# Gated slot attention block on one core: a second home for the high and low halves of two head weights, made one and two slots before the change of head

## What is computed

```
q = silu(causal_conv4(h @ Wq));  k, v, w likewise            # 16 heads of 128
g = log_sigmoid(h @ Wf1 @ Wf2);  beta = sigmoid(h @ Wb);  w = l2norm(w)
scan over the 512 tokens, per head:
    Sk = Sk * exp(g) + k (beta w)^T ;  Sv = Sv * exp(g) + (beta w) v^T
    o  = softmax(q Sk / sqrt(128)) Sv
o = rms_norm(o) * norm_w * sigmoid(h @ Wg1 @ Wg2 + bg2)
x = layernorm(x + o @ Wo);  x = layernorm(x + ffn(x))
```

## Time and profile before

| what | value |
|---|---|
| median of three executions | 2012.46 us |
| the profiled execution, device time | 2009.03 us |
| its span in the profile | 2007.3 us |
| PE busy | 1927.6 us, 96% |
| PE weight loads | 1627.1 us, 81% |
| DVE busy | 1775.8 us, 88% |
| ACT busy | 1396.5 us, 70% |
| POOL busy | 1334.0 us, 66% |
| chain that ended last, by engine | PE 82%, POOL 8%, DVE 5%, issue 3%, ACT 1%, DMA 1% |
| granted TensorE clock, mean | 0.984 of full speed |

### The profile page before, as it was taken

One profiled execution on the slowest core, in us unless ns is written; L12 is line 12 of the kernel. 1 busy time (PEld: TensorE's weight loads), 2 busy tenths in 40 slices (PEclk: granted clock), 3 DMA queues, 4 the chain that ended last, 5 costly groups with the idle time before them and its releaser, 6 DMA issues.

```text
span 2007.3 us, 41500 instructions
## 1 busy us (share of the span) xinstructions
PE 1927.6 (96%) x12192; PEld 1627.1 (81%) x12192; DVE 1775.8 (88%) x4096; ACT 1396.5 (70%) x3986; POOL 1334.0 (66%) x2289
## 2 busy tenths in 40 slices
PE   7899999999999999999999999999999999999697
PEld 5688888888888888888888888888888888887586
DVE  5599999999999999999999999999999999998487
ACT  4477777777777777777777777777777777776442
POOL 5367676767677676777677776777676766766343
PEclk8899999999999999999999999999999999999798
DMA  3011110111111111111111111111110111102300
GB/s 78 1 55 26 25 35 14 36 24 33 26 24 26 26 34 23 27 24 32 26 27 23 27 34 24 26 24 33 26 34 15 29 32 23 22 15 51 63 11 32
DMA packets 53645, 58.51 MB, mean 29 GB/s; under 512 B 14896, under 2 KB 44720, under 8 KB 53424
## 3 DMA queue, kind: packets, MB, share of 16 engines
q0 software_dynamic: 9216, 33.56, 11.4%
q1 hardware_dynamic: 44208, 22.29, 4.0%
HBM read 20.19 MB, written 37.75 MB: 29 GB/s over the span
## 4 chain that ended last, share of the span: by engine, by line
PE 82%; POOL 8%; DVE 5%; issue 3%; ACT 1%; DMA 1%; POOLq 0%; DVEq 0%; ACTq 0%
PE proj_ps L718 15%; PE mix_ps L802 11%; PE V_ps L773 10%; PE work_ps L927 8%; PE work_ps L933 7%; PE tr_ps L742 6%; PE V_ps L751 5%; PE work_ps L1569 5%; PE proj_ps L397 4%; PE work_ps L822 3%; PE mix_ps L809 2%; POOL w_lo L370 2%; PE tr_ps L782 2%; PE work_ps L824 2%; POOL qk L618 1%
## 5 line engine op out<-in xcount | busy, mean ns | idle before, releaser
L587 DVE SCALAR_TENSOR_TENSOR conv<-proj_ps,coefs,conv 128x511 f32<-128x511 f32 (+2 forms) x768 | 561.9, 732 | 9.5 <-ACT conv L347 2.6
L298 POOL TENSOR_TENSOR W<-W,tot 128x256 f32<-128x256 f32 x384 | 256.0, 667 | 244.0 <-PE mix_ps L802 243.9
L1053 POOL TENSOR_TENSOR A_lev<-A,masks 128x256 f32<-128x256 f32 x448 | 319.5, 718 | 0.1
L802 PE MATMUL mix_ps<-W,U 128*128 128x128 f32 x1792 | 295.3, 287 | 13.7 <-POOL W L298 8.2
L802 PEld LDWEIGHTS mix_ps<-W,U 128*128 128x128 f32 x1792 | 256.5, 192 | 40.2 <-issue 24.5
L773 PE MATMUL V_ps<-A_lev,UT 128*128 128x128 f32 x1792 | 285.9, 282 | 1.6 <-DVE V_ps L683 1.6
L711 DVE COPY_PREDICATED A<-masks,mix_ps 128x256 f32<-128x256 uint32 x448 | 268.7, 600 | 12.3 <-PE mix_ps L802 12.2
L580 DVE TENSOR_TENSOR wT<-wT,tot 128x128 f32<-128x128 f32 x768 | 233.3, 344 | 40.3 <-DVE U L563 1.8
L773 PEld LDWEIGHTS V_ps<-A_lev,UT 128*128 128x128 f32 x1792 | 237.4, 192 | 23.4 <-DVE V_ps L683 23.2
L356 ACT ACTIVATE th<-conv 128x512 f32<-128x512 f32 x256 | 162.3, 634 | 104.2 <-DVE conv L587 103.0
L718 PE MATMUL proj_ps<-hT_hi,w_hi 128*128 128x512 f32 x512 | 222.9, 435 | 4.5 <-DVE conv L587 2.7
(11 more groups left out here) (200 smaller groups left out, 4774.0 us busy)
## 6 DMA issues: line engine op xcount, KB each, us to landing
head_sum<-y_sb POOLq DMA_DIRECT2D x64, 512.0 KB, 6.5
w_raw<-in_L_attn_Ww SPq DMA_DIRECT2D x16, 128.0 KB, 2.2
w_raw<-in_L_attn_Wq SPq DMA_DIRECT2D x16, 128.0 KB, 2.2
w_raw<-in_L_attn_Wk SPq DMA_DIRECT2D x16, 128.0 KB, 2.3
w_raw<-in_L_attn_Wv SPq DMA_DIRECT2D x16, 128.0 KB, 2.2
wo_raw<-in_L_attn_Wo SPq DMA_DIRECT2D x16, 128.0 KB, 2.0
head_sum<-in_L_attn_hidden_states SPq DMA_DIRECT2D x1, 2048.0 KB, 10.3
acc<-head_sum SPq DMA_DIRECT2D x4, 512.0 KB, 3.9
```

The costliest lines, as they stand in the source:

```text
L298: nc.gpsimd.tensor_tensor(w, w, block_tot(u3.par, lev, 0), ALU.mult).then_inc(W_step, 1)
L587: nc.vector.scalar_tensor_tensor(y_, proj_ps[:, CONV_BANK[i], 0:T - back], filt(u, i, KW - 1 - back), y_, ALU.mult, ALU.add).then_inc(conv ...
L802: last = nc.tensor.matmul(mix_ps[:, half, p * P:(p + 1) * P], Ulev(u3, lev)[:, p * P:(p + 1) * P], after_odd(W[:, p * T // 2:(p + 1) * T / ...
L1053: nc.gpsimd.tensor_tensor(dst, diag_after_odd(lev), mask_cols(lev), ALU.mult)\
```

## The change

For odd heads the halves of Ww and Wq (i < 2) live in the first 512 columns of `setup_hi_sb` and `setup_lo_sb`; for even heads in `w_hi` and `w_lo` as before. The two homes alternate, so the halves of the next head can be made while the present head is still in use. Ww's halves are now made in the slot n % 4 = 1, two slots sooner than before, and Wq's in the slot n % 4 = 2, one slot sooner; for head 1 both are made in slot 2, when the first products are done. ACT makes the high half at r = 3 as before, POOL the low half after `fac` as before. The halves of Wf2 and Wk stay where they were, in the slot n % 4 = 3, that of Wv in the slot n % 4 = 0. Two waits guard the buffers: on `proj_ps_ready` for the end of head h-2, and for head 1 on `raw_ps`.

```
+        def half(main, other, h, i):
+
+            if h % 2 and i < 2:
+                return other[:, i * KT * P:(i + 1) * KT * P].rearrange("p (k n) -> p k n", k=KT)
+            return main[:, i]
+
         def high_weights(act, h, i):
 
             act.wait_ge((head_w, head_q, head_k, head_v)[i], 16 * (h + 1))
-            nc.scalar.activation(w_hi[:, i], w_raw[:, i], ACT.Copy).then_inc(high_done, 1)
+            if h and i < 2:
+                wait(act, proj_ps_ready, 5 * B * (h - 1))
+            if h == 1 and i == 0:
+                act.wait_ge(raw_ps, B)
+            nc.scalar.activation(half(w_hi, setup_hi_sb, h, i), w_raw[:, i], ACT.Copy).then_inc(high_done, 1)
 
         def low_weights(pool, h, i):
 
             pool.wait_ge(high_done, 4 * h + i + 1)
-            nc.gpsimd.tensor_tensor(w_lo[:, i], w_raw[:, i], w_hi[:, i].bitcast(F32),
+            nc.gpsimd.tensor_tensor(half(w_lo, setup_lo_sb, h, i), w_raw[:, i], half(w_hi, setup_hi_sb, h, i).bitcast(F32),
                                     ALU.subtract).then_inc(low_done, 1)
+
+        def ahead(s):
+
+            if not s.u1 or s.u1.h + 1 == H:
+                return ()
+            return {1: (0,) if s.u1.h else (), 2: (1,) if s.u1.h else (0, 1)}.get(s.u1.par, ())
...
-            split_product(proj_ps[:, CONV_BANK[i], :], w_hi[:, i], w_lo[:, i],
+            split_product(proj_ps[:, CONV_BANK[i], :], half(w_hi, setup_hi_sb, u.h, i), half(w_lo, setup_lo_sb, u.h, i),
...
+                for i in ahead(s):
+                    low_weights(pool, u1.h + 1, i)
                 if s.next_h:
-                    low_weights(pool, s.next_h, 0)
                     low_f(pool, s.next_h)
-                    low_weights(pool, s.next_h, 1)
                     low_weights(pool, s.next_h, 2)
...
+                    if r == 3:
+                        for i in ahead(s):
+                            high_weights(act, u1.h + 1, i)
                     if s.next_h and r == 3:
                         act.wait_ge(proj_ps_ready, u1.count(5, 3))
                         high_f(act, s.next_h)
-                        high_weights(act, s.next_h, 0)
-                        high_weights(act, s.next_h, 1)
```

## The result

The changed kernel took 2016.39 us (median of 12 executions, 2014.26 to 2018.48), the kernel before 2012.16 us (12 executions on the same chips, 2008.47 to 2014.18). The ratio is 1.0022, with a 95% interval of 1.0013 to 1.0031. The profiled execution took 2014.42 us (span 2012.7), that of the kernel before 2009.03 (span 2007.3).

A forecast was written before the change was run, and what follows sets the result against it. DVE, its scalings and copies held up by POOL, was taken to decide slot length at L751 behind a change of head. Terms of 3.5 + 0.7 = +4.2 us on the median 2012.46 gave 2016.6 us, range 2010.8 to 2019.5.

The forecast's parts named there:

- slot 20: First slot of head 5, 28.33 us before; forecast like other changes of head, with L751 at +0.25 us.
- slot 56: Slot behind a change of head, 28.63 us before; already has such a collision, so L751 was to change by -0.04.
- POOL is free at once, and the wait for qk goes: At a new head, L618 starts 0.17 us into the slot; PE's 15 waits of 0.43 us go.
- The wait is worth only 0.05 us a head: At each change of head, taking away PE's wait for qk alone would win 0.05 us, not 0.34.
- The pair is held up and DVE comes 0.30 us later: New head's start: scaling pair L580 falls behind POOL's q product; taps start at 600.88 instead of 600.58.
- L751 at +0.25 us for 14 heads, 3.5 us: PE's second product into V_ps starts at 605.70 instead of 605.45 in slot 20; +3.5 us for 14 changes of head.
- Slots n % 4 = 3, +0.7 us: `w_lo` at the end of slots n % 4 = 2 makes `largest` about 0.2 us late; 0.05 us for each of 15.
- ACT and SP at nothing: ACT's high halves in slots n % 4 = 1 and 2 are covered, SP's order stays; no cost counted.
- The wait for qk was the bound: Rival: at changes of head L751 goes back to 9.07 us; -5.4 us, 2007.1 us; chance 0.11.
- The pair gets in first: Rival: DVE's first scaling passes before L618, taps start as now; between -0.8 and +0.7 us, 2012.5 us; chance 0.20.
- The halves are not made sooner: Rival: a raw weight or a wait comes late, so POOL waits for ACT; about 2012.5 us; chance 0.02.

The follow-up runs named there:

- Ww only: The changed kernel, but only Ww's halves are made early and Wq's stay in the slot n % 4 = 3: 2010.69 us, ratio 0.9999 to the kernel before.
- the gate products alone: The kernel before, with the gate products of levels 4 and 5 made at i == 4, except in slots n % 4 = 2: 2008.65 us, ratio 0.9985.
- the order alone: The kernel before, with DVE's scaling of level 3 put ahead of `largest` at the change of head: 2018.88 us, ratio 1.0038.
- The first experiment: The changed kernel, with DVE's scaling of level 3 put ahead of `largest` at the change of head: 2005.77 us, ratio 0.9976 to the kernel before.
- three fillers: The changed kernel plus three POOL instructions writing an unread spare tile, at the end of the slot before a new head: 2012.24 us, ratio 1.0003 to the kernel before.
- the two fillers: The changed kernel plus two POOL instructions writing an unread spare tile, in place of the two `w_lo` taken away: 2015.69 us, ratio 1.0027 to the kernel before.

## Why the prediction was right, point by point

**The total.** Forecast 2016.6 us, measured 2016.39 against 2012.16; +4.2 us forecast over the kernel before, +4.2 measured between the medians. That the two agree so closely is in part luck, since the interval of the ratio allows 2.6 to 6.2 us. In the profiled executions the difference is 5.4 us, and the slots, +5.6 together, show what the sum had wrong: slot 20 costs 0.9 us more than I gave it, slot 56 0.2 more, the slots n % 4 = 1 and 2, which I had at nothing, 0.6, and the slots n % 4 = 3 0.3 less. The mechanism is the forecast one: the held pair makes up 3.3 us of it, in the 13 changes of head other than those at slots 20 and 56.

**POOL is free at once, and the wait for qk goes.** Right: L634 at 0.17 us, L943 at 2.62, no wait. **The wait is worth only 0.05 us a head.** Right: 0.04 us in the experiment with Ww only, and 4.79 - 4.73 = 0.06 in the table.

**The pair is held up and DVE comes 0.30 us later.** Right: 1.54 us for a forecast of 1.53; "DVE done" goes from 4.62 to 4.92. What the prediction didn't say is that the kernel before already lost 0.76 us there to the same two instructions; it was contained in the measured start of the taps, so the sum held. Had I listed it, the likely gain of another order would have been plain: the pair only has to be ahead of the q product. The Trainium skill, SBUF — State Buffer, section "SBUF: two separate sides", has whole instructions wait in turn for a pair of ports, and the traces agree: what is held ends about 0.14 us behind the half of the q product that it waited for. With the gate products alone, a half that ends at 712.02 + 0.75 = 712.77 gives 712.91, and the copy ends at 712.04 + 0.87 = 712.91; in the changed kernel 711.08 + 1.48 + 0.14 = 712.70, and the pair ends at 712.72. It holds through the whole trace of the kernel before: between 118 and 1900 us every one of the 103 scalings that start while a 128 by 256 instruction of POOL has more than 0.2 us to run ends 0.14 to 0.16 us behind its end, and the 139 such copies 0.14 to 0.20 us. The small gate products, which the prediction has holding nobody up, do the same; they are only so short that little comes of it (with the order alone, a scaling that starts at 715.63 under one that ends at 715.81 takes 0.32 us for 0.29).

**L751 at +0.25 us for 14 heads, 3.5 us.** Nearly right: 9.64 for 9.66. The 13 slots other than 20 and 56 are longer by 0.26 us each, 3.3 us together; slot 56 by 0.12 instead of -0.04. PE's wait there was 0.67 us and not 0.85: I let all the lateness gather at L751, but the weight load ahead of it waits 0.30 us (0.12 in slot 20 before) for ACT's copy of UT_top. That copy stands in ACT's queue behind L356, which waited 0.67 us for DVE's late taps.

**Slot 20** was the term that I missed, +1.18 us instead of +0.25. The prediction says that DVE runs without a gap from the start of the slot to L711, and in slot 20 that isn't so. The stop of 0.46 us cost nothing before, and now adds itself and pushes the last scaling onto POOL's W. I had read slot 20 as a slot like the others, from its start and its L751.

**Slots n % 4 = 3, +0.7 us** (0.05 each). Not confirmed as a mechanism: the late `largest` came, its cost didn't. `largest` did lose its cover at the end of slots n % 4 = 2: it started 27.69 us into slot 22 with no wait, where it had waited 0.29 us; but its slots are longer by 0.025 us, no more than those of n % 4 = 1, which I had set to nothing and which are longer by 0.02 too. All three kinds without a change of head together are +1.0 us in this one execution. The first experiment, with the same halves at the same places, has them at 28.01, 27.85 and 28.00 us, so the halves themselves don't cost it; where it comes from stays open.

**ACT and SP at nothing.** Nothing speaks against it: with three fillers, all of the change but its effect on the q product is in, and the ratio is 1.0003.

**The rivals.** *The wait for qk was the bound* is refuted by Ww only. *The pair gets in first* didn't happen here, since the q product started at 0.17 and the pair at 0.27 us into the slot in all heads; with a start at 0.56 us, after the pair's, it gets in, a copy and the next pair are held instead, and the time is that of the kernel before, as this rival had it. *The halves are not made sooner*: the weight loads of head 5 read `setup_lo_sb` in slot 20 without a wait.

## What to carry to other kernels

When work is taken off an engine, what follows it on that engine comes sooner and may meet other work of the engine that it holds up, as POOL does DVE here; ask what stands in that place on the other engine, to a tenth of a microsecond. A wait that vanishes from the list proves nothing: look for the instruction that held the same consumer as the next to last. Where such a change loses a little, don't drop it before the order on the other engine is tried with it: here the two edits cost 0.2% and 0.4% alone and gain 0.24% together.

## What the runs showed of the hardware that was not expected

- A later start on POOL made a faster kernel: with the q product at 1.14, 1.54 and 0.56 us into the slot the slots took 28.61, 28.39 and 28.29 us. Whether POOL's A_lev is 0.10 us ahead of DVE's copy or 0.14 us behind it decides 0.46 us (the copy of 0.79 or 0.33 us).
- Instructions of one shape on POOL took different times: the two fillers, equal in all, 0.73 and 0.66 us, the `w_lo` of the same size, which reads two tiles and not one, 0.78 behind them. A filler isn't a stand-in to a tenth.
- DVE stops for 0.46 us with nothing to wait for, near 235, 398, 599, 963 and 1407 us of the kernel before. In all ten kernels it stops ahead of the same five instructions, counted from the start of DVE's program (0.46 to 0.48 us each). In all 50 cases the profile has a DMA of the kind `instruction`, of 8 KB, that begins 1.12 to 1.43 us after the stop does. That points to the loading of DVE's program, but no run here changes that loading, so the cause isn't shown.
